# A selective scan with a mixture of experts: four banks for the decays, one for the spread of B

## The reference

```python
xn = _rmsnorm(x, rms_w)
xr = xn @ W_in
xs, res = jnp.split(xr, 2, axis=-1)          # 512 channels each
xs = jax.nn.silu(causal_conv4(xs) + conv_b)
x_ssm = xs @ W_x
dt, Bm, Cm = jnp.split(x_ssm, [D_INNER, D_INNER + D_STATE], axis=-1)
dt = jax.nn.softplus(dt @ W_dt)
A = -jnp.exp(A_log)
A_disc = jnp.exp(A[None, None] * dt[..., None])
Bx = dt[..., None] * Bm[:, :, None, :] * xs[..., None]

def step(h, inp):
    Ad_t, Bx_t, C_t = inp
    h = Ad_t * h + Bx_t
    y = jnp.einsum('bdn,bn->bd', h, C_t)
    return (h, y)
...
y = y * jax.nn.silu(res)
out = y @ W_out
return residual + out
```

## Time and profile before

| | |
|---|---|
| median of 3 runs | 2478.15 us (2477.71 to 2479.02) |
| the profiled execution | 2483.63 us, its span 2481.9 us |
| first to last scan | 156.2 to 2207.6 us of the span |
| busy: VectorE, GpSimd, TensorE, ScalarE | 77%, 76%, 69%, 52% |
| mean granted clock of TensorE | 0.839 of full speed |

### The profile page before, as it was taken

The page is one execution under the profiler, slowest core; times in us unless marked ns, Lnnn a source line. Parts: engine busy times, 40 slices in busy tenths (PEclk is TensorE's granted clock), DMA queues, the critical chain, the costliest instruction groups (busy, mean ns, idle before and its releaser), DMA issues. The chain is left out here.

```text
span 2481.9 us, 22825 instructions
## 1 busy us (share of the span) xinstructions
PE 1721.2 (69%) x5716; PEld 673.0 (27%) x5716; DVE 1921.6 (77%) x2445; ACT 1297.0 (52%) x2050; POOL 1878.4 (76%) x634
## 2 busy tenths in 40 slices
PE   5777868586868767686868686868696874451770
PEld 2222323232222223232323231323232220110670
DVE  2058989888889798898989898988888889865202
ACT  2246565656555656565656566565656555431111
POOL 0059897978888878797988888897979788960556
PEclk9888989798898979898989898989898885665895
DMA  2084525244444334243434342525344343302852
GB/s 97 18 240 87 126 55 127 59 106 91 102 95 102 86 90 102 72 106 74 112 85 111 85 112 65 124 54 124 70 105 91 93 95 94 85 9 78 297 155 70
DMA packets 135466, 245.16 MB, mean 99 GB/s; under 512 B 25536, under 2 KB 77514, under 8 KB 135232
## 3 DMA queue, kind: packets, MB, share of 16 engines
q1 hardware_dynamic: 129472, 233.83, 37.9%
q0 software_dynamic: 5888, 10.29, 1.8%
HBM read 78.92 MB, written 31.13 MB: 44 GB/s over the span
## 5 line engine op out<-in xcount | busy, mean ns | idle before, releaser
L797 DVE TENSOR_TENSOR_SCAN h<-pa,carry,bq 128x512 f32<-128x512 f32 x1024 | 1261.7, 1266 | 118.8 <-ACT pa L660 117.6
L925 POOL TENSOR_TENSOR h<-h,c_rep 128x2048 f32<-128x2048 f32 x256 | 1157.4, 4530 | 192.0 <-DVE carry L802 191.9
L660 ACT ACTIVATE pa<-rep,neg_a 128x512 f32<-128x512 f32 x1024 | 694.9, 687 | 578.2 <-DVE h L797 576.9
L393 PE MATMUL pp<-xnt,w_c 128*128 128x512 f32 x1024 | 529.1, 660 | 73.5 <-ACT xs L572 48.2
L918 POOL TENSOR_TENSOR bq<-rep,b_rep 128x2048 f32<-128x2048 f32 x96 | 433.8, 4519 | 82.8 <-DVE h L797 80.3
L371 PE MATMUL py<-h,blk 128*32 128x512 f32 x2048 | 319.6, 697 | 251.2 <-DVE gate L808 217.7
L783 DVE TENSOR_TENSOR bq<-rep,pb 128x2048 f32<-128x2048 f32 x160 | 361.9, 2262 | 26.4 <-PE pb L428 26.4
L419 PE MATMUL pp<-xs,w_dtx 128*128 128x512 f32 x512 | 273.8, 669 | 74.8 <-DVE du L726 63.3
L393 PEld LDWEIGHTS pp<-xnt,w_c 128*128 128x128 f32 x1024 | 198.1, 205 | 370.9 <-issue 252.7
L400 PE MATMUL pp<-xnt,w_res 128*128 128x512 f32 x256 | 146.6, 700 | 75.2 <-DVE du L726 44.1
L371 PEld LDWEIGHTS py<-h,blk 128*32 128x32 f32 x2048 | 43.8, 116 | 463.3 <-issue 214.2
(11 more groups left out here) (157 smaller groups left out, 1591.7 us busy)
## 6 DMA issues: line engine op xcount, KB each, us to landing
rep<-du SPq DMA_DIRECT2D x1024, 128.0 KB, 2.4
c_rep<-bc_scratch SPq DMA_DIRECT2D x64, 256.0 KB, 4.8
combine_scratch<-zeros SPq DMA_DIRECT2D x16, 520.0 KB, 7.7
xt<-in_L_attn_x_dram SPq DMA_DIRECT2D x16, 512.0 KB, 3.6
b_rep<-bc_scratch SPq DMA_DIRECT2D x64, 128.0 KB, 3.5
xo<-in_L_attn_x_dram SPq DMA_DIRECT2D x16, 512.0 KB, 3.6
out_dram<-z SPq DMA_DIRECT2D x16, 512.0 KB, 3.0
hidden_scratch<-late SPq DMA_DIRECT2D x16, 512.0 KB, 3.3
```

The source lines that it names most:

```text
L393: mm = pe.matmul(pp[:], w_c[:, k, tap, m * P:(m + 1) * P], xnt[:, k, tap:tap + T], start=(n == 0 and tap == 0), stop=(n == 3 and tap == 3))
L660: act.activation(pa[:, decay_bank(t), :], rep[:, c % 2, t % 4, 0, :], ACT.Exp, scale=neg_a[:, a_column(t):a_column(t) + 1]).then_inc(s_exp, 1)
L797: v.tensor_tensor_scan(h[:, quad % 4, t % 4, :], pa[:, decay_bank(t), :], bq[:, quad % 2, t % 4, :], carry[:, par, t:t + 1], ALU.mult, ALU ...
L925: pool.tensor_tensor(h[:, quad % 4], h[:, quad % 4], c_rep[:, par, quad % 4, :].unsqueeze(1).broadcast_to((P, 4, T)), ALU.mult).then_inc(s ...
```

## The change

`pa` gets a fourth bank, taken from `pb`, which keeps one. Unit t uses bank t % 4 and waits for scan t - 4, without exceptions. AHEAD becomes 3, so that ScalarE at slot t does `decays(t + 3)`. The one bank `pb` is filled once for each of the ten quads of VectorE, at the slots `SEL`: 59 and 63 of the step before, and 7, 15, 23, 31, 39, 47, 51, 55 of the tile's own. Each spread waits for VectorE's previous `inputs`, and each `inputs` waits for its spread. In the weight products of the setup the two banks of `pb` are replaced by the banks 2 and 3 of `pa`.

```diff
-AHEAD = 2
+AHEAD = 3
...
-SPREADS = ((0, 0, 0, 15), (2, 1, 2, 14), (1, 0, 13, 12), (3, 0, 15, 13))
+SEL = (59, 63, 71, 79, 87, 95, 103, 111, 115, 119)
...
 def decay_bank(t):
-    return 1 if t == UNITS - 1 else t % 3
+    return t % 4
...
-        pa = ps("pa", [P, 3, T])
-        pb = ps("pb", [P, 2, T])
+        pa = ps("pa", [P, 4, T])
+        pb = ps("pb", [P, T])
...
-                    for n, (g, bank, quad, before) in enumerate(SPREADS):
-                        if t == PREP["sel"][n]:
-                            pe.wait_ge(s_free, NU * i + use("bc") + 1)
-                            atleast(pe, s_bd, NV * (i - 1 if before > quad else i) + made_by(VECTOR_QUADS, before + 1))
+                    for n, quad in enumerate(VECTOR_QUADS):
+                        if t == SEL[n]:
+                            if n == 0:
+                                pe.wait_ge(s_free, NU * i + use("bc") + 1)
+                            atleast(pe, s_bd, NV * i + n)
                             b = 32 * par
-                            pe.matmul(pb[:, bank, :], sel_b[b:b + 32, g, :], bc[b:b + 32, :], start=True, stop=True,
-                                      tile_position=(b, 0)).then_inc(s_brep[n], 1)
+                            pe.matmul(pb[:], sel_b[b:b + 32, quad % 4, :], bc[b:b + 32, :], start=True, stop=True,
+                                      tile_position=(b, 0)).then_inc(s_brep, 1)
...
-                    atleast(act, s_scan, UNITS * i + bank_before(t) + 1)
+                    atleast(act, s_scan, UNITS * i + t - 3)
...
-                    for n, (group, bank, first, _) in enumerate(SPREADS):
-                        if group == g:
-                            pb_bank = bank
-                            if quad == first:
-                                v.wait_ge(s_brep[n], i + 1)
+                    v.wait_ge(s_brep, NV * i + made_by(VECTOR_QUADS, quad) + 1)
                     atleast(v, s_scan, UNITS * i + 4 * quad - 4)
                     v.tensor_tensor(bq[:, quad % 2], rep[:, c % 2, :, 1, :],
-                                    pb[:, pb_bank, :].unsqueeze(1).broadcast_to((P, 4, T)), ALU.mult).then_inc(s_bd, 1)
+                                    pb[:].unsqueeze(1).broadcast_to((P, 4, T)), ALU.mult).then_inc(s_bd, 1)
```

More of the change, by code:

```diff
@@ L43 @@
     pe_xs=((-19, -18, -17, -16), (-13, -12, -11, -10), (-7, -6, -5, -4), (-1, 0, 1, 2)), act_xs=(-13, -7, -1, 5), silu_x=5,
-    pe_bc=(7, 8), act_bc=10, store_bc=11, load_c=12, load_b=60, sel=(58, 55, 111, 115),
+    pe_bc=(7, 8), act_bc=10, store_bc=11, load_c=12, load_b=60,
     pe_dt=((11, 12), (17, 18), (22, 23), (36, 37)), abs=(14, 21, 25, 39), exp=(15, 22, 26, 40), o1=(16, 23, 28, 41),
@@ L221, in scan_layers @@
         s_xs, s_sg = sem("xs_ready"), sem("gate_ready")
-        d_bcs, d_crep, d_brep, s_brep = (sem("bc_stored"), sem("c_loaded"), sem("b_loaded"),
-                                         [sem(f"b_spread_{n}") for n in range(len(SPREADS))])
+        d_bcs, d_crep, d_brep, s_brep = sem("bc_stored"), sem("c_loaded"), sem("b_loaded"), sem("b_spread")
         s_abs, s_sp, s_o1, s_ln, s_s, s_o2 = (sem("softplus_abs"), sem("softplus_exp"), sem("softplus_head"),
@@ L516, in _ @@
                             for j in range(DC):
-                                mm = pe.matmul(pb[:, k % 2, :], wxt[:, j, k * P:(k + 1) * P], wdt[:, j, :],
+                                mm = pe.matmul(pa[:, 2 + k % 2, :], wxt[:, j, k * P:(k + 1) * P], wdt[:, j, :],
                                                start=(j == 0), stop=(j == DC - 1))
@@ L528, in _ @@
                         pe.wait_ge(s_wpc, DC)
-                    if t == PREP["sel"][1]:
+                    if t == SEL[0]:
                         pe.wait_ge(s_sel, 2)
@@ L586, in prep @@
                         atleast(act, d_bcs, 16 * i)
-                        for n in range(len(SPREADS)):
-                            atleast(act, s_brep[n], i - 1)
+                        atleast(act, s_brep, NV * (i - 1))
                         act.copy(bc[32 * par:32 * par + 32, :], pp[32 * par:32 * par + 32, :]).then_inc(s_free, 1)
@@ L694, in _ @@
                             act.wait_ge(s_wp, 1 + k)
-                            act.copy(w_dtx[:, k, :], pb[:, k % 2, :]).then_inc(s_wpc, 1)
+                            act.copy(w_dtx[:, k, :], pa[:, 2 + k % 2, :]).then_inc(s_wpc, 1)
                         act.wait_ge(s_arow, 1)
```

## The result

The changed kernel takes 2486.23 us (median of 12 runs, 2483.74 to 2488.12), the kernel before 2479.76 us beside it. The ratio is 1.0026, with a 95% interval of 1.0017 to 1.0035: slower by about 6.5 us, where 6.3 us faster had been forecast. The time lies inside the range of 2449 to 2488 us, on the wrong side.

The account below looks back on a forecast made before the run. The prediction held chains passing between engines to bound the kernel, no engine being full. Nine tiles gaining 0.70 us, five losing 0.2 and 1 us before the loop gave 6.3 us: 2471.8 us, range 2449 to 2488.

Parts of the forecast that it names:

- (a) The lead in stretch 1: Slot 56 to slot 8 of the next tile: the fourth decay bank and AHEAD 3 gain 1.25 us.
- (a) Stretch 4: Slot 35 to inputs of quad 13: 1.22 us gained at slot 45, lost to quad 13's spread wait; gain zero.
- (b) Slots 63, 7, 15, 31, 39: One-bank spreads there: 0.1 us lost at 63, 0.3 us given back at 15, nothing at 7, 31, 39.
- (b) Slot 59: Spread behind `xs` matmuls delays next tile's first inputs at most 0.5 us, under a 3.99 us wait: nothing.
- (b, c) Slot 23: Spread between halves of a `dt` group: 0.15 to 0.2 us lost; about 1.07 us late in slow-clock tiles.
- (c) The count of slow tiles: TensorE's slow clock at the `dt` group: 5 slow tiles 0.2 us worse each, 9 others gaining 0.70 us each.
- Rival 3: Slower, chance 0.17: slot 23's spread inside a 1.2 GHz `dt` group in every tile, VectorE waiting at slot 28; 2491 us.
- Rival 2: TensorE gets faster, chance 0.20: six spreads fill idle time, speeding slow groups; 2447 us, or 2460 us for half.

## Why the prediction was wrong, step by step

**(a) The lead in stretch 1: the direction right, the size by luck.** 1.25 less 0.1 us was worked out, 1.14 us was measured in tile 8, 0.97 us a tile in the thirteen tiles, and the wait stands at slot 9. The decay waits were forecast at about 70 us and are 58.0. But two errors meet in this number. Where no spread is waited for at slot 61 the lead is worth 2.0 us or more (31.8 to 29.8 us a tile): the prediction looked at scan 8 alone, and in the kernel before VectorE also waits 1.42 us at scan 2 or 0.47 us at scan 4, which the lead takes away too. The other error is slot 59, below.

**(a) Stretch 4: half right.** That the gain at slot 45 is handed on to the inputs of quad 13 was right: their wait is 1.5 to 3.1 us, in all spread waits 50.3 us (forecast: over 40). That it nets zero was nearly so: the stretch is 0.97 us shorter in tile 8, but 0.35 us in the mean of thirteen tiles. What was not seen is how much this zero held back. Moving one spread by one slot gave 55 us, 26 us of it in this stretch. The prediction took the spread at slot 47 as fixed by Ln; but TensorE runs the four matmuls of slot 46 before it, about 2 us, which need not stand there (the expectation above says eight; it is four).

**(b) Slots 63, 7, 15, 31, 39: right.** At slot 63 the last `xs` group starts at 1189.60 instead of 1189.47. The wait for `out` at slot 15 is 0.21 us where 0.3 had been set. From tile 1 on the inputs wait for spreads at slots 49 and 61 only.

**(b) Slot 59: a term put at nothing that was not nothing.** The bound of 0.5 us was read from tile 8 of the kernel before, where the slow clock ahead of this spread is short: TensorE's `xs` group of slot 57, the sum behind it and the next group take 3.46, 1.23 and some 1.8 us. In the step from tile 8 to 9 of the changed kernel they take 3.78 (at 1306.98), 1.94 and 2.22 us, the spread ends at 1315.83, and the inputs of slot 61 wait 1.57 us (1.58 us at most elsewhere). Nor is the wait covered: scan 9 waits 3.93 us behind a wait of 0.30 us at slot 61 and 3.79 us behind one of 1.57 us. The stretch up to scan 9 takes 29.8 us in the two tiles without that wait, 30.6 to 30.8 us in five with 0.3 or 0.4 us, and 31.8 to 32.0 us in six with 1.4 to 1.6 us. Against 29.8 us everywhere that is 17 us. The trace with the spread at slot 46 agrees: no wait, and 29.8 or 29.9 us in each of the thirteen tiles. In it the slow clock at slot 57 is gone too, so no run parts the spread's place at slot 59 from the clock there.

**(b, c) Slot 23: mis-sized.** It was set at 0.15 to 0.2 us in 9 tiles and 1.07 us in 5. Measured, there are 14 waits at slot 28 from 300 us on, of 1.43 to 3.15 us, 31.9 us in all. With the spread at slot 24 they are 9.3 us less; what stays, 22.6 us, comes with the slow dt group.

**(c) The count of slow tiles: the step that failed.** Nine fast and five slow tiles were carried over, as if the pattern belonged to the tile. The five were worked out from periods; the trace itself has seven slow groups at slot 22 in these 14 tiles, and seven fast ones. In the changed kernel none is fast. In the seven tiles that had been fast the forecast set 0.70 us gained each, 4.9 us. Measured from scan 56 to scan 56 they take 915.1 us instead of 907.8, so 1.04 us each were lost, 7.3 us. It was lost between scan 9 and slot 35, 2.4 us a tile and 16.8 us in all, where less than 0.5 us a tile had been set; the two other stretches gained 9.5 us. Together these 12.2 us are more than the 10.8 us by which the profiled execution missed the forecast in its frame (2488.1 against 2477.3). A slow tile was set 0.2 us worse; the six tiles from 2 to 14 that were slow already are 5.4 us better in all.

Why the group at slot 22 became slow in every tile stays open. What the traces show is the order of events: in the seven tiles the group at slot 17 now runs at 2.4 GHz, TensorE is done earlier and waits 3.9 us instead of 2.2 at slot 22, and the group there runs at 1.2 GHz, for most or all of its length. The spread at slot 15 is not the reason, since the kernel with one spread a tile has the same pattern, and the 3.9 us of idle time are not needed, since the group stays slow behind 1.13 us.

**Rival 3 is what happened, in the main.** Its place, the spread at 1.2 GHz inside the group and VectorE waiting for Exp were right. Its deciding point, idle time of 3.90 us, goes along with the slow group but is not its cause. Its price was a little high (2491 us against 2486), and its chance of 0.17 too low. That price was worked out without the 17 us of slot 59 and without the larger worth of the lead, so how close it came is partly luck. The two signs that were to show the prediction wrong, decay waits under 40 us and a clock moved by more than 0.02, did not come (58.0 us, 0.010); the sign that mattered was where the slow clock stands.

**Rival 2, TensorE getting faster, fell.** Six more spreads filled idle time, and the mean granted clock went from 0.839 to 0.829. The rule of the Trainium skill, page "TensorE: Matmul & The Clock Gate", section "What's actually happening", that activity releases the slow clock, was read there as "more matmuls help". The kernel with three spreads in the gap shows that this reading is too simple: 1.13 us of idle, and a granted clock of 0.50 all the same. What sets the moment of the slow clock was not found.

## What to carry to other kernels

A wait that is taken away shows its worth only after the next wait behind it has been looked at as something that can be moved; here the lead was worth 24 us with the spreads where they stood, and 51 us with two of them moved by one slot. When an operation is put into the queue of an engine with gaps, try it beside a group that somebody waits for and not between its halves; here that was 15 us. A wait is not covered because a longer one follows on the same engine: look whether the later one shrinks when the earlier one grows. And do not carry a clock pattern from one trace to another kernel: price a group on the critical chain at the slow clock in every tile, and at the fast one, and let the range hold both.

## What the runs showed of the hardware

Two things had not been expected. The slow clock of TensorE can come after 13 us of nearly full work (granted 1.00 with 12.92 of 13.60 us busy, then 0.50 from the start of 1.13 us of idle through the whole next group). And where it sits can change by itself: in the kernel before it moved from slot 22 to slot 17 at tile 7, without any change in the program, and the tiles became 1.9 us shorter (130.47 and 132.51 us in turn, then 129.62 us); in tile 14 it was back at slot 22.
